# Attention and int8 layer on one core: unrolled program, rounds in pairs, output transposed by head group, values projected late

## The reference

```python
x = normalise(x * s1)                       # s1, s2: the two halves of cond, per batch
q, k = (x @ Wq.T) * q_dc, (x @ Wk.T) * k_dc
v    = (x @ Wv.T) * v_dc * s2
attn = softmax(q @ k.T / 4)                 # 16 heads of 16 features
out  = (attn @ v) @ Ww.T * w_dc + (v @ Wu.T) * u_dc
q_lhs = round(out / lhs_scale)              # int8 by row, lhs_scale = absmax / 127
q_rhs = round(rhs / rhs_scale)              # int8 by column
y = (q_lhs @ q_rhs) * lhs_scale * rhs_scale
return x_in + y
```

## Time and profile before

| stage (us from the span's start) | us | granted PE clock |
|---|---|---|
| prologue, to the first scores (0 to 51.08) | 51.08 | 0.93 |
| step 0 (51.08 to 99.81) | 48.73 | 0.93 |
| step 6, the last turn of the loop (380.51 to 432.99) | 52.48 | 1.00 |
| step 7 (432.99 to 472.63, end of the last exponential) | 39.64 | 1.00 |
| whole span | 494.9 | 0.96 |
| profiled execution | 496.59 | |
| median of three runs | 498.12 | |

### The profile page before, as it was taken

One profiled execution on the slowest core, in us unless ns is written; L12 is line 12 of the kernel. 1 busy time (PEld: TensorE's weight loads), 2 busy tenths in 40 slices (PEclk: granted clock), 3 DMA queues, 4 the chain that ended last, 5 costly groups with the idle time before them and its releaser, 6 DMA issues.

```text
span 494.9 us, 8739 instructions
## 1 busy us (share of the span) xinstructions
PE 447.1 (90%) x2626; PEld 225.3 (46%) x2626; DVE 241.7 (49%) x564; ACT 290.1 (59%) x333; POOL 103.6 (21%) x124
## 2 busy tenths in 40 slices
PE   6892899979999999969999999969999999999982
PEld 5771235434554455524454455424554455544251
DVE  4766142346444763446434763447444763444054
ACT  4030587556765766637765766647765766677930
POOL 5442003010121303031121303031121303020022
PEclk9997699998999999979999999989999999999997
DMA  6068309660497209650397209660497209620021
GB/s 208 0 149 176 68 1 137 109 146 1 62 129 159 88 20 134 107 177 0 57 130 145 105 12 139 107 182 0 64 128 158 87 22 135 106 88 1 1 86 42
DMA packets 29804, 45.31 MB, mean 92 GB/s; under 512 B 3928, under 2 KB 15448, under 8 KB 29704
## 3 DMA queue, kind: packets, MB, share of 16 engines
q1 hardware_dynamic: 27840, 40.02, 45.6%
q0 software_dynamic: 1072, 3.74, 1.9%
q10 hardware_dynamic: 832, 0.80, 0.5%
HBM read 15.09 MB, written 4.28 MB: 39 GB/s over the span
## 4 chain that ended last, share of the span: by engine, by line
PE 78%; issue 5%; ACT 5%; DMA 5%; DVE 5%; SPq 2%; POOL 1%; POOLq 0%; ACTq 0%; DVEq 0%
PE o_acc L953 22%; PE scores L939 16%; PE work L976 10%; PE work L997 9%; PE work L815 8%; PE work L1087 6%; ACT probs L493 4%; PE work L985 3%; DMA q_stack<-const_dram 2%; PE work L844 2%; PE work L1101 1%; DMA x_res<-in_L_cond_w_weight_dram 1%; DVE o_nat L749 1%; DMA rows<-in_cond_dram 1%; SPq L322 1%
## 5 line engine op out<-in xcount | busy, mean ns | idle before, releaser
L493 ACT ACTIVATE probs<-scores 128x1024 f32<-128x1024 f32 x256 | 247.9, 1026 | 129.0 <-PE scores L939 128.8
L953 PE MATMUL o_acc<-probs,v_aug 128*32 128x512 f32 x1024 | 140.7, 622 | 0.2
L939 PE MATMUL scores<-q_stack,k_stack 50*128 50x512 f32 x512 | 103.2, 467 | 26.7 <-DMA q_stack<-const_dram 10.9
L939 PEld LDWEIGHTS scores<-q_stack,k_stack 50*128 50x128 f32 x512 | 41.0, 191 | 81.9 <-issue 37.2
L420 POOL TENSOR_TENSOR squares<-parts 128x512 bf16<-128x512 f32 x32 | 33.3, 1041 | 185.5 <-ACT parts L473 185.5
L976 PE MATMUL work<-x_t,qk_w 128*128 128x512 f32 x192 | 54.3, 421 | 0.0
L997 PE MATMUL work<-vs_w,x_t 128*128 128x512 f32 x192 | 50.9, 407 | 0.3 <-DVEq L680 0.3
L439 POOL TENSOR_TENSOR res<-res,x_res 128x512 f32<-128x512 f32 x16 | 20.0, 1270 | 136.6 <-DVEq L799 136.6
L976 PEld LDWEIGHTS work<-x_t,qk_w 128*128 128x128 f32 x192 | 35.2, 193 | 24.1 <-issue 6.7
L997 PEld LDWEIGHTS work<-vs_w,x_t 128*128 128x128 f32 x192 | 34.2, 188 | 23.4 <-issue 13.9
L953 PEld LDWEIGHTS o_acc<-probs,v_aug 128*32 128x32 f32 x1024 | 20.5, 109 | 49.1 <-issue 45.5
(11 more groups left out here) (110 smaller groups left out, 389.4 us busy)
## 6 DMA issues: line engine op xcount, KB each, us to landing
q_stack<-parts SPq DMA_DIRECT2D x96, 128.0 KB, 5.3
k_stack<-parts SPq DMA_DIRECT2D x96, 128.0 KB, 5.5
x_sb<-in_x_dram SPq DMA_DIRECT2D x8, 512.0 KB, 5.4
x_res<-in_x_dram SPq DMA_DIRECT2D x8, 512.0 KB, 3.9
out_dram<-res POOLq DMA_DIRECT2D x7, 512.0 KB, 4.7
rows<-rows_dram SPq DMA_DIRECT2D x8, 384.0 KB, 5.5
rows<-in_cond_dram SPq DMA_DIRECT2D x8, 128.0 KB, 5.3
q_stack<-const_dram SPq DMA_DIRECT2D x16, 32.0 KB
```

The source lines that it names most:

```text
L493: nc.scalar.activation(probs[:, r % 2, pair:pair + 2, :], scores[:, pair:pair + 2, :], ACT.Exp).then_inc(exp_done, 1)
L939: last = nc.tensor.matmul(scores[:, 2 * (u % 2) + e, :], k_stack[top:top + ROWS, par, 2 * g + u % 2, kt * P:(kt + 1) * P], q_stack[top:top ...
L953: last = nc.tensor.matmul(o_acc[DV * j:DV * (j + 1), :], v_aug[:, par, kt, 4 * g + j, :], probs[:, r % 2, j, :], start=(kt == 0), stop=(kt ...
```

## The change

- The loops are written out. Every semaphore value, bank and buffer is a constant, and all uses of the `work` banks stand in one list (`ORDER`).
- Two rounds form a group (`SUPER` = 8 in a step). PE's order in a group is: scores of r, values of r - 2 and of r - 1, scores of r + 1, one fill. `probs` has three buffers instead of two. A fill now holds the work of about two of the old ones (`step_fills`), and every group has one.
- The output of a head group is transposed to tokens as soon as it is complete: "on" 0, 1, 2 in groups 3, 5 and 7 of the same step, 3 in group 0 of the next. DVE's `normalise` follows for each.
- Values: key tile 0 of batch a is projected in the last group of step t, tiles 1 to 3 in the first two groups of step t + 1. `v_aug` has one buffer. So the prologue has one value projection instead of four, and step 7 gets three.
- "ffn" and the rest of a batch end one step later than before (batch t - 2 in step t); the last step takes "ffn" of batches 5 and 6.
- The zeros go into `q_stack` at the start of each step (`zero_shift`), without waiting for the flag; with a small bound SP only adds to the semaphore (`load_shift`). In the prologue this and the ones for `k_stack` are issued before the demodulation rows.
- The norms' transposition (`norms_transposed`) opens the last fill of the step, and the jump over the row maxima closes it.
- Behind the last batch only one "on" is left; both "yqt" come before both "ffn".

```diff
-        probs = sb("probs", [P, 2, 4, S])
+        probs = sb("probs", [P, RING, 4, S])
...
-        v_aug = sb("v_aug", [P, 2, KT, NH, DV])
+        v_aug = sb("v_aug", [P, KT, NH, DV])
...
+    ffn = [[("ffn", y, n)] if y >= 0 else [] for n in range(2)]
+    return [[("v", t, 1), ("v", t, 2), ("on", z, 3)],
+            [("v", t, 3), ("xt", a, 0), ("xt", a, 1)],
+            [("ot", z, 0), ("q", a, 0), ("k", a, 0)],
+            [("ot", z, 1), ("on", t, 0), ("q", a, 1)],
+            ffn[0] + [("k", a, 1), ("y", z, 0)],
+            ffn[1] + [("on", t, 1), ("fold", a, 0)],
+            [("yqt", z, 0), ("y", z, 1), ("norms", a, 0)],
+            [("v", a, 0), ("on", t, 2), ("yqt", z, 1)]]
...
-                for r in range(ROUNDS):
-                    scores_of(t, par, r, has_z)
-                    if r > 0:
-                        values_of(t, par, r - 1, has_z)
-                    elif has_z:
-                        values_of(t - 1, 1 - par, ROUNDS - 1, True)
-                    if r in fills:
-                        fills[r]()
+            for t in range(B):
+                for i in range(SUPER):
+                    r = t * ROUNDS + 2 * i
+                    scores_of(r)
+                    if r > 0:
+                        values_of(r - 2)
+                        values_of(r - 1)
+                    scores_of(r + 1)
+                    fill(t, i)
...
+            def load_shift(a):
+
+                wait(flag_ready, a + 1)
+                small = sp.value_load(flag[0:1, 0:1], min_val=0, max_val=1)
+                with sp.If(small == 1):
+                    sp.sem_inc(shift_loaded, SHIFT)
...
+            sp.wait_ge(pool_stored, 16)
+            zero_shift(0)
```

More of the change, by code:

```diff
@@ L202, in adaln_ffn_kernel @@
         spare = sem("spare")
[L205 to L234, removed]
-                for odd in range(2):
-                    t = pair * 2 + (1 + odd)
-                    step(t, (1 + odd) % 2, has_a=True, has_z=True, base=uses_before(t), bank=uses_before(1 + odd))
-            if tally is not None:
-                tally.end_loop(PAIRS)
-            step(B - 1, (B - 1) % 2, has_a=False, has_z=True, base=uses_before(B - 1), bank=uses_before(B - 1))
-        LAST_Z = uses_before(B - 1) + Z_USES
-        LAST_AT = {use: LAST_Z + n for n, use in enumerate(
-            [("on", q) for q in range(KT)] + [("ot", 0), ("ot", 1), ("y", 0), ("y", 1), ("yqt", 0), ("ffn", 0),
-                                              ("yqt", 1), ("ffn", 1)])}
         block = ctx.enter_context(nc.Block())
@@ L514, in _ @@
         @block.vector
         def _(dve):
-            chain = Tally(dve_step)
+            chain, taken = Tally(), Tally()
             def link(instruction):
@@ new lines, in norms, with norms_transposed @@
+            def norms(a):
+                pe.wait_ge(squares_ready, a * 4 + 4)
+                bank = claim("norms", a, 0)
+                for n in range(4):
+                    last = nc.tensor.matmul(bank[32 * n:32 * (n + 1), :], head_ones[:, :], squares[:, n, :],
+                                            start=True, stop=True)
+                last.then_inc(norms_summed, 1)
+            def norms_transposed(a):
+                pe.wait_ge(norms_ready, a + 1)
+                bank = work[:, USE[("norms", a, 0)] % NW, :]
+                transpose(bank[0:1, 0:P], norm_max[:, :]).then_inc(work_ready, 1)
@@ new lines, in _ @@
+            bank = claim("sums", 0, 0)
+            for m in range(5):
+                pe.wait_ge(w_sq_ready, m + 1)
+                style = 0 if m <= WV else HC
+                for g in range(HC):
+                    for c in range(HC):
+                        last = nc.tensor.matmul(bank[:, (m * HC + g) * B:(m * HC + g + 1) * B],
+                                                w_sq[:, m, c, g * P:(g + 1) * P], cond_sq[:, style + c, :],
+                                                start=(c == 0), stop=(c == HC - 1))
@@ new lines, in _ @@
+            last.then_inc(work_ready, 1)
+            x_transposed(0, 0)
+            x_transposed(0, 1)
+            pe.wait_ge(demod_ready, 1)
+            for n, ms in enumerate(((WV, WW), (WU,))):
+                bank = claim("rows", 0, n)
+                for i, m in enumerate(ms):
+                    for g in range(HC):
+                        last = transpose(bank[0:B, i * H + g * P:i * H + (g + 1) * P], demod[:, m * HC + g, :])
+                last.then_inc(work_ready, 1)
+            for _ in range(4):
+                nc.tensor.matmul(scores[:, 0, 0:P], ones[:, :], ident[:, :], start=True, stop=True)
```

1262 lines of the change are left out of this document (676 added, 586 removed).

## The result

The changed kernel took 459.89 us (median of 4 runs, 458.79 to 460.3) against 498.49 us for the kernel before beside it (4 runs, 497.38 to 499.31): a ratio of 0.922, 95% interval 0.920 to 0.925. The forecast was 465 us, with a range of 456 to 482. The profiled run took 460.14 us, with a span of 458.1.

The account below looks back on a forecast made before the run. PE's instructions were taken to bound each step. Prologue, steps 0 to 7 and tail summed to 457.6 us; 3.7 for jumps made 461.3 of span, and 1.7 and 1.5 above it 464.5, given as 465 (range 456 to 482).

Parts of the forecast that it names:

- entries: On PE, entering a fill from another kind of matmul costs 0.19 us; 8 entries a step instead of 15 gain 1.3.
- the loop's returns: Returns to the loop's top: 4.51 us standing still, then 7.05 at clock 0.53; steps 1 to 6 took 18 more.
- Stalls behind jumps: PE's sequencer stalls after the jump at a step's end, 1.85 us each; two of seven places counted, 3.7.
- rival (a): No jump stalls at the steps' ends: 461 us; with the prologue a little shorter too, 455 to 461, chance 0.17.
- The wait for the norms' maximum: At a step's end PE waits 0.35 us (bounds 0 and 1) for DVE, which quantises y's second half first.
- The jump: At a step's end, flag, sequencer work and waits take 3.0 us against 2.35 of queued work: PE stands still 0.65.
- A steady step: Steps 2 to 6: 49.4 us of PE work plus 1.0 of step-end waits, 50.4 each against 52.48 before.
- the 0.90: Cost in us of each value product in a pair, instead of 1.00; nothing lower held possible; gains 0.8 a step.
- Step 7: Last step: 40.1 us of PE work, 0.5 for ACT-paced groups, 0.7 for the last exponentials: 41.3.
- Prologue: Before the first scores: zeros and ones go out early, SP's 24 stack transfers come next; first scores at 45.5, not 51.08.
- step 0: First step: 42.3 us of PE work plus waits, half-clock value projections and the jump: 48.5.
- Values late: First batch's value projections moved from the prologue into step 0: 3.1 us charged for two at half clock.

Follow-up runs that it names:

- the unrolled one: The kernel before with its loop over pairs of steps written out as straight-line code, order, fills and prologue as before: 482.29 us, ratio 0.970.
- e9_early_flag: Changed kernel with POOL's scaling mid-step, norms maximum before y's second-half quantisation, flag made inside it, norms transposed before the step's last scores: 458.13 us, ratio 0.923.

## Why the prediction was right, and where it was off

**The main line held.** PE bounds a step; entries cost 0.19 (0.18 to 0.21 measured); the loop's returns were a large loss (15 measured, 18 read); the first scores follow SP's issuing. The sum, 464.5, was 4.6 above the median: 3.2 in the span, and 1.4 in what lies around it, 2.04 instead of 1.7 for the profiled run, and a median 0.25 below that run where I added 1.5.

**Stalls behind jumps, 3.7, were none.** This is the term that failed, and rival (a) had it right. The step that failed is taking a gap from inside the loop as a property of the jump. The Trainium skill's rule that I set against it (Runtime: NRT & Kernel Launch, Instruction fetch mechanics: a branch stalls only where it leaves its window) agrees with these traces: none of 14 jumps in straight-line code, seven in the changed kernel and seven in the unrolled one, shows it. Whether the window is the cause in the loop, no run here shows.

**The wait for the norms' maximum, 0.35, was 0.79.** I took the quantisation's 3.05 from step 6 before, beside which POOL did nothing then; in the new place POOL's scaling runs beside it and it takes 3.6. The mechanism, DVE late by its own order, was right. **The jump, 0.65, was 0.42**: from the norms' transposition to the next scores it is 3.03 (240.96 to 243.99), as summed, but the work queued between took 2.6 instead of 2.35. The two waits are separate as long as the maximum stands behind the quantisation (with POOL moved the first fell to 0.23 and the second stayed at 0.22 to 0.48); with the maximum ahead, the second grew to 0.8. Together they were forecast at 1.0 and came to 1.2.

**A steady step, 50.4, was 49.98.** The pair at 1.85 instead of 1.90 gives 0.4 of it. The second product of a pair adds 0.86, so the 0.90 that I called the least was not.

**Step 7, 41.3, was 43.25.** I gave its short fills 4.1 a group, the pace of ACT alone. The last full groups of the changed kernel, PE's timeline:

```profile
424.80 0.73 PE L887 MATMUL scores<-q_stack,k_stack 50*128 50x512 f32 x4
...
426.49 0.49 PE L887 MATMUL scores<-q_stack,k_stack 50*128 50x512 f32 x2
427.33 0.51 PE L887 MATMUL scores<-q_stack,k_stack 50*128 50x512 f32 x2 [0.35 <-ACT probs L473]
427.77 1.92 PE L901 MATMUL o_acc<-probs,v_aug 128*32 128x512 f32 x16
429.62 0.74 PE L887 MATMUL scores<-q_stack,k_stack 50*128 50x512 f32 x4
```

and ACT's:

```profile
425.34 3.77 ACT L473 ACTIVATE probs<-scores 128x1024 f32<-128x1024 f32 x4 [1.05 <-PE scores L887]
```

A group takes 4.82 (424.80 to 429.62): the pair waits for the second round's exponentials, and ACT then waits 1.05 for the scores behind the pair. The pair is in the chain between two exponentials here, and three groups lose about 0.7 each by it: 2.1, against the 1.95 that the step was short. That is the other side of the match above.

**Prologue, 45.5 to 46.59, and step 0, 48.5 to 47.94,** half cancel.

**Values late** was no gain for the first batch: I counted 3.1 for two projections at half clock in step 0 as a price of the change, but not that PE stood still for 7 us in the prologue where they were free. Moved back they gave 3.8 in step 0.

## What to carry to other kernels

Where one engine feeds another that needs a fixed time (here 1.9 us of exponentials for each round), look at what stands behind each producer: it should be as much other work as the consumer takes. Pairs with whole fills met this in a steady step and pairs with cut fills did not (49.98 against 54.8), although the cut itself cost only 1.3 in changes of kind. A stall seen inside a hardware loop says little about the same branch in straight-line code. Before an edit to one of two waits in a row, ask what the second will be once the first is gone: single edits at the end of a step gained 0.42 to 0.48 each, and two of them together 0.55. A flag that is made earlier helps only if nothing that stands ahead of its reading is late.

## What the hardware did that I had not expected

- DVE's passes from memory to memory ran longer beside POOL: 0.39 instead of 0.17, 0.84 instead of 0.62 for two, 0.55 instead of 0.43; its reciprocal beside them, 0.17, did not.
- From PE's wait for the flag to the next scores its sequencer takes 1.6 to 1.8 us (287.84 to 289.57 in e9_early_flag), of which the load of one value is 0.30. Queued work hid it where there was enough (step 0 of e9_early_flag), and 1.0 us of transposes did not.
- A value product alone takes 0.99 and two take 1.85.
- Issuing the same transfers from two engines moved the limit to landing, 8.72 instead of 5.5.
